# The depthwise convolution of q, k and v on TensorE instead of VectorE, in a macaron block on eight cores

## The chip, the cores and the metric

The kernel runs on all 8 cores of one Trainium2 chip. Each core takes one of the 8 batch elements, runs the same program and exchanges nothing with the others. A time is the device time of the slowest core in microseconds. A core has five engines with an instruction stream each (TensorE, VectorE, ScalarE, GpSimdE, SyncE); they meet only through semaphores. Weights and activations are moved by DMAs, which SyncE, ScalarE or GpSimdE issue.

## The reference

One batch element is x of 2048 x 1024. Three residual steps follow one another: half a feed-forward layer, gated delta attention, half the same feed-forward layer again.

```python
x = x + 0.5 * ffn(layernorm(x))        # complex 512x512 matrix built from two tensor-train cores
x = x + attn(layernorm(x))
x = x + 0.5 * ffn(layernorm(x))

def attn(x):                           # T=2048, D=1024, H=16 heads of 64
    q, k, v = x @ Wq.T, x @ Wk.T, x @ Wv.T
    q, k, v = causal_depthwise_conv(q, cq_w, cq_b), ...   # 4 taps for each channel, plus bias
    g, beta = log_sigmoid(x @ Wg.T), sigmoid(x @ Wb.T)
    k = k / norm(k);  q = q * 64 ** -0.5
    for t:                             # for each head, S is 64x64
        delta = outer(v_t, k_t) - outer(S k_t, k_t)
        S = exp(g_t) * S + beta_t * delta
        o_t = S q_t
    return o @ Wo.T
```

The change concerns only the second line of `attn`: `y[c, t] = b[c] + sum over j of w[c, j] * x[c, t - 3 + j]`, for 1024 channels of each of q, k and v.

## The kernel before

The program is unrolled and written in one order; each operation is put on its engine's stream with the events it must wait for. The helper `mm` (L250) puts out every matmul and the helper `dma` (L273) every DMA. Each finished instruction adds one to its engine's semaphore: `ET` for TensorE, `EV` for VectorE, `EA` for ScalarE, `EP` for GpSimdE. `s.now(ET)` is the number that `ET` will have when everything put on TensorE's stream so far is done, so a wait for it is a wait for all TensorE work written ahead of that place.

After the first feed-forward stage, the second layer norm and the gates, the attention runs over 4 slabs of 512 time steps. A slab has four steps: `_slab_qkv` (projections and convolution), `_slab_prep` (8 chunks of 64 steps), `_slab_solve` and `_slab_chain` (the recurrence and the output projection, with weights `woT`).

`_slab_qkv` works through 24 tiles: q, k, v, each with 8 tiles `ct` of 128 channels. A tile is

- at an even `ct`, a DMA from GpSimdE's queue of 512 KB of weights, which serve this tile and the next, into one of two ring buffers `wring`. It waits for `s.now(ET)`;
- 8 matmuls of 128x128 by 128x512 into PSUM tile `pp0` or `pp1` in turn. The first waits for the weights and for `s.now(EV)`, `s.now(EP)` and `s.now(EA)` (`dep0`);
- the convolution: VectorE copies the last 3 columns of the slab before from `tails` (L648), copies PSUM to `rawt` in fp32 (L650) and saves the new last 3 columns (L652); ScalarE makes the tap of shift 0 with bias into `cacc` (L659); VectorE adds the other three taps (L662, L665, L668) and casts the sum to bf16 into the strip `qcs`, `kcs` or `vcs` (L671).

Weights and bias of a channel stand in one column each (`c_convw`, `c_convb`), read as an operand of one value per partition.

`_slab_prep` begins on ScalarE's queue with three small DMAs (`tcols2` twice, `lgT2`); VectorE splits `lgT2` into three bf16 parts `lgs` (L718 to L726), TensorE spreads them over `pp3` (24 matmuls), and transposes `kcs` into `pp2`.

Of the kernel before, what the change touches and what calls it, by code (L numbers as in the profile page):

```python
# [9 lines left out]
BF16 = mybir.dt.bfloat16  # L10
AF = mybir.ActivationFunctionType
ALU = mybir.AluOpType
# [95 lines left out]
def hr(h):  # L108
    return 64 * (h % 2)


class MK:
# [47 lines left out]
    def _declare_sbuf(self):  # L160
# [60 lines left out]
        self.msk = self._alias("msk", (128, 512), F32, self.ovl3, 4096)  # L221
        self.sstb = self._alias("sstb", (128, 4 * 256), BF16, self.ovl3, 4096)
        self.ktmb = self._alias("ktmb", (128, 512), BF16, self.ovl2, 4096)
        self.subtmp = self._alias("subtmp", (128, 4 * 16 * 15), BF16, self.ovl3, 6144)
        self.msk2 = self._alias("msk2", (128, 512), F32, self.ovl3, 6144)
        self.rbt = self._alias("rbt", (128, 512), F32, self.ovl4, 0)
# [386 lines left out]
    def _slab_qkv(self, sl):  # L613
        s = self.s
        ev_x2 = self.dma(QS, self.x2s[:],
                         self.scr_x2t[:, :, sl * 512:(sl + 1) * 512]
                         .rearrange("a p c -> p a c"),
                         deps=tuple(self.ev_x2t[sl * 4:sl * 4 + 4]) + (s.now(ET),))
        strips = {"q": self.qcs, "k": self.kcs, "v": self.vcs}
        wbase = {"q": 0, "k": 4, "v": 8}  # L620
        self.ev_strip = {}
        ev_conv_last = None
        for wi, w in enumerate("qkv"):
            wsrc = self.wT[w].rearrange("(j p) c -> p j c", p=128)
            ev_w = {}
            for ct in range(8):
                qt = ct // 2
                slot = self.wring[qt % 2]
                if ct % 2 == 0:
                    ev_w[qt] = self.dma(  # L630
                        QG, slot[:].rearrange("p (j cc) -> p j cc", j=8),
                        wsrc[:, :, qt * 256:(qt + 1) * 256],
                        deps=(s.now(ET),))
                pb = self.pp[ct % 2]
                dep0 = (ev_x2, ev_w[qt], s.now(EV), s.now(EP), s.now(EA))
                ev_last = None
                for j in range(8):
                    c0 = j * 256 + (ct % 2) * 128
                    ev_last = self.mm(
                        pb[:, 0:512], slot[:, c0:c0 + 128],  # L640
                        self.x2s[:, j * 512:(j + 1) * 512],
                        deps=dep0 if j == 0 else (), start=(j == 0), stop=(j == 7))
                tl = self.tails[:, (wi * 8 + ct) * 3:(wi * 8 + ct) * 3 + 3]
                dpre = [ev_conv_last]
                if wi == 0 and ct == 0:
                    dpre += [s.now(ET), self.ev_lgflat, self.ev_tcols,
                             s.now(EV), s.now(EA)]
                e_pref = self.dve(lambda e, tl=tl: e.tensor_copy(self.rawt[:, 0:3], tl),  # L648
                                  deps=dpre)
                e_raw = self.dve(lambda e, pb=pb: e.tensor_copy(  # L650
                    self.rawt[:, 3:3 + 512], pb[:, 0:512]), deps=(ev_last,))
                self.dve(lambda e, tl=tl: e.tensor_copy(tl, self.rawt[:, 512:515]),  # L652
                         deps=(e_raw, e_pref))

                def wc(j_, ct=ct, w=w):
                    cix = ct * 12 + wbase[w] + j_
                    return self.c_convw[:, cix:cix + 1]
                bc = self.c_convb[:, ct * 3 + wi:ct * 3 + wi + 1]
                e_c0 = self.act(lambda e, wc=wc, bc=bc: e.activation(  # L659
                    self.cacc[:], self.rawt[:, 3:515], AF.Identity, bias=bc, scale=wc(3)),  # L660
                    deps=(e_pref, e_raw, self.ev_cs))
                e_c1 = self.dve(lambda e, wc=wc: e.scalar_tensor_tensor(  # L662
                    self.cacc[:], self.rawt[:, 2:514], wc(2), self.cacc[:],
                    ALU.mult, ALU.add), deps=(e_c0,))
                e_c2 = self.dve(lambda e, wc=wc: e.scalar_tensor_tensor(  # L665
                    self.cacc[:], self.rawt[:, 1:513], wc(1), self.cacc[:],
                    ALU.mult, ALU.add), deps=(e_c1,))
                e_c3 = self.dve(lambda e, wc=wc: e.scalar_tensor_tensor(  # L668
                    self.cacc[:], self.rawt[:, 0:512], wc(0), self.cacc[:],
                    ALU.mult, ALU.add), deps=(e_c2,))  # L670
                ev_sp = self.dve(lambda e, w=w, ct=ct, strips=strips: e.tensor_copy(  # L671
                    strips[w][:, ct * 512:(ct + 1) * 512], self.cacc[:]), deps=(e_c3,))
                self.ev_strip[(w, ct)] = ev_sp
                ev_conv_last = ev_sp
        self.ev_strip_done = ev_conv_last
# [17 lines left out]
    def _slab_prep(self, sl):  # L693
# [13 lines left out]
        bd = getattr(self, "bankdep", {})  # L707
        ppK, ppV = self.pp[2], self.pp[3]
        for chl in range(SLAB):
            ch = sl * SLAB + chl  # L710
            ev_tc2a = self.dma(QA, self.tcols2[chl % 2][0:64, :], self.scr_tc[ch],
                               deps=(self.ev_tcols,) + tuple(self.ev_tc2rd[chl % 2]))
# [4 lines left out]
                              deps=(self.ev_lgflat,) + tuple(self.ev_lgt_rd))  # L717
            e_h = self.dve(lambda e: e.tensor_copy(self.lgs[:, 0:64], self.lgT2[:]),  # L718
                           deps=(ev_lgt, self.ev_bc_prev))
            e_h = self.dve(lambda e: e.tensor_sub(  # L720
                self.lgT2[:], self.lgT2[:], self.lgs[:, 0:64]), deps=(e_h,))
            e_h = self.dve(lambda e: e.tensor_copy(self.lgs[:, 64:128], self.lgT2[:]),
                           deps=(e_h,))
            e_h = self.dve(lambda e: e.tensor_sub(
                self.lgT2[:], self.lgT2[:], self.lgs[:, 64:128]), deps=(e_h,))
            e_h = self.dve(lambda e: e.tensor_copy(self.lgs[:, 128:192], self.lgT2[:]),  # L726
                           deps=(e_h,))
            self.ev_lgt_rd = (e_h,)
            ev_bc = None
            for pa in range(8):  # L730
                for k3 in range(3):
                    ev_bc = self.mm(
                        ppV[:, pa * 64:pa * 64 + 64],
                        self.c_selb[:, pa * 128:(pa + 1) * 128],
                        self.lgs[:, k3 * 64:k3 * 64 + 64],
                        deps=(e_h, self.ev_ppV_rd, bd.get("pO2"))
                        if pa == 0 and k3 == 0 else (),
                        start=(k3 == 0), stop=(k3 == 2))
            self.ev_bc_prev = ev_bc
            ev_lgrow = self.act(lambda e: e.activation(self.lgrow[:], ppV[:], AF.Copy),  # L740
                                deps=(ev_bc,) + tuple(self.ev_lgrd))
            ev_lg = (ev_lgrow,)
            ev_kt = []
            for h in range(H):
                r0 = hr(h)
                dep = (self.ev_strip[("k", h // 2)],)
                if h == 0:
                    dep += (self.ev_ppK_rd, bd.get("pO1"))
                ev_kt.append(self.mm(
                    ppK[r0:r0 + 64, (h // 2) * 64:(h // 2) * 64 + 64],  # L750
                    self._kc(h, chl, self.kcs), self.c_i64d[r0:r0 + 64, :],
                    deps=dep, tp=(r0, r0)))
            ev_ktmb = self.dve(
                lambda e: e.tensor_copy(self.ktmb[:], ppK[:]),
                deps=(ev_kt[-1], s.now(ET)) + tuple(self.ev_ktm_rd) if chl == 0
                else (ev_kt[-1], self.ev_kc_prev) + tuple(self.ev_ktm_rd))
            ev_sq = self.act(lambda e: e.activation(self.ksq[:], ppK[:], AF.Square),
                             deps=(ev_ktmb, self.ev_ksq_rd))
# [14 lines left out]
                deps=ev_lg + (ev_lnrn,))  # L773
            ev_ms, ev_Es, ev_khs, ev_ts, rdt = [], [], [], [], []
            for par in range(2):
                def tc(c0, par=par, chl=chl):
# [5 lines left out]
                    deps=ev_tc2 + (ev_lnrn,))  # L782
# [3 lines left out]
                                 deps=(ev_m,))  # L786
                ee3 = self.dve(lambda e, cp=cp: e.tensor_scalar_mul(cp(2), cp(8), -1.0),
                               deps=(ev_e1,))
# [4 lines left out]
                    bias=self.cst[par * 64:par * 64 + 64, 2:3]), deps=(ev_lnrn,))  # L793
# [7 lines left out]
                               deps=(ee4,) + ev_lg)  # L801
# [10 lines left out]
                deps=tuple(ev_khs) + (ev_ktmb,))  # L812
# [5 lines left out]
                deps=(ev_rn, self.ev_kc_prev if chl else s.now(ET)))  # L818
            ev_kc = None
            for h in range(H):  # L820
# [6 lines left out]
                    deps=(ev_dgr, ev_ktmb, ev_sq) if h == 0 else (), tp=(r0, r0))  # L827
# [6 lines left out]
            for h in range(H):  # L834
                r0 = hr(h)
                dep = (self.ev_strip[("v", h // 2)],)
                if h == 0:
# [4 lines left out]
                    deps=dep, tp=(r0, r0)))  # L842
# [3 lines left out]
            for h in range(H):  # L846
# [4 lines left out]
                    deps=(ev_kce,) if h == 0 else (), tp=(r0, r0))  # L851
            for h in range(H):
# [4 lines left out]
                    deps=(ev_vtm,) if h == 0 else (), tp=(r0, r0))  # L857
# [10 lines left out]
                deps=ev_lg + tuple(ev_ms) + (s.now(EV),))  # L868
# [3 lines left out]
                          deps=(e3,))  # L872
            e5 = self.dve(lambda e, chl=chl, mskt=mskt, ppK=ppK: e.tensor_mul(
                self.mps2[chl % 2][:], mskt[:], ppK[:]),
                deps=(e4, ev_g) + tuple(self.ev_mp_out[chl % 2]))
# [6 lines left out]
                          deps=(f2,))  # L882
# [457 lines left out]
```

How the kernel before makes its waits and increments, by code:

```python
    def replay(self, eng_name, eng):  # L98
        for item in self.prog[eng_name]:
            if item[0] == "w":
                eng.wait_ge(self.sems[item[1]], item[2])
            elif item[0] == "i":
                item[1](eng).then_inc(self.sems[item[2]], item[3])
            else:
                item[1](eng)
```

## Time and profile before

| | us |
|---|---|
| median of 3 runs | 4031.08 (4020.88 to 4033.50) |
| profiled execution, its own time | 4025.85 |
| span of its slowest core | 4024.0 |
| spans of the eight cores | 3994.8 to 4024.0 |
| PE busy | 1249.0 (31%) |
| DVE busy | 1336.4 (33%) |
| ACT busy | 420.5 (10%) |
| POOL busy | 232.1 (6%) |

PE is TensorE's matmuls, PEld its weight loads, DVE VectorE, ACT ScalarE, POOL GpSimdE, SP SyncE; ACTq is the issue of a DMA by ScalarE. The mean granted clock of TensorE was 0.559 to 0.562 of full speed on every core, where 0.5 is 1.2 GHz and 1.0 is 2.4 GHz. No engine is busy for more than a third of the span. Slab 1, from which most rows below are, has its 24 tiles between 1353 and 1583 us; over the four slabs there are 96 tiles.

### The profile page before, as it was taken

How to read it: one execution, taken by the hardware profiler on the slowest of the kernel's cores; microseconds unless marked ns; L12 is line 12 of the kernel's file. 1: busy time of each engine (PE TensorE's matmuls, PEld its weight loads, DVE VectorE, ACT ScalarE, POOL GpSimd, SP SyncE). 2: the span in 40 equal slices, each digit the busy share in tenths (PEclk: the TensorE clock that was granted, in tenths of full speed). 3: DMA queues.
4: the chain of work that ended last, by engine and by line, in shares of the span. 5: the costliest groups of instructions: out<-in, count | busy, mean ns of one | idle time of the engine just before them, and what ended most of it. 6: DMA issues, size and time to landing. Idle time of an engine off the chain costs nothing.

```text
span 4024.0 us, 35646 instructions; the slowest of 8 cores (3994.8 to 4024.0 us)
## 1 busy us (share of the span) xinstructions
PE 1249.0 (31%) x12112; PEld 619.4 (15%) x12112; DVE 1336.4 (33%) x2703; ACT 420.5 (10%) x1161; POOL 232.1 (6%) x314
## 2 busy tenths in 40 slices
PE   1553323311243333113343321033333210343254
PEld 0121001111121111102120111031101110221011
DVE  2222213444521244453122444531134444321221
ACT  0225100021000001210000011000000110000021
POOL 2000000000100000001000000100000001000100
PEclk9775555555555555555555555555556555555576
DMA  4002112201612221015213210332222108112102
GB/s 129 0 0 53 34 28 26 27 8 11 19 27 37 47 27 23 8 10 20 42 27 47 27 19 9 23 9 37 37 42 27 15 10 24 19 30 37 42 1 84
DMA packets 284802, 114.94 MB, mean 29 GB/s; under 512 B 203280, under 2 KB 260768, under 8 KB 284608
## 3 DMA queue, kind: packets, MB, share of 16 engines
q0 software_dynamic: 139504, 70.91, 17.1%
q1 hardware_dynamic: 112224, 32.70, 3.5%
q10 hardware_dynamic: 32896, 9.05, 1.1%
q8 instruction: 100, 1.64, 0.2%
q14 instruction: 78, 0.64, 0.1%
HBM read 147.46 MB, written 26.08 MB: 43 GB/s over the span
## 4 chain that ended last, share of the span: by engine, by line
PE 30%; DVE 25%; DMA 23%; issue 12%; ACT 6%; ACTq 2%; POOL 1%; DVEq 1%; SPq 1%; POOLq 0%
PE pp L250 30%; DMA wring<-woT 8%; DMA wring<-wqT 2%; DMA wring<-wvT 2%; DMA wring<-wkT 2%; DVE subtmp L946 2%; DMA scr_tc<-tcst 1%; ACTq L273 1%; DMA lgT<-scr_flat 1%; ACT cacc L659 1%; DVE cacc L953 1%; ACT xTt L458 1%; DVE cacc L662 1%; DVE cacc L665 1%; DVE cacc L668 1%
## 5 line engine op out<-in xcount | busy, mean ns | idle before, releaser
L250 PE MATMUL pp<-x2s,wring 128*128 128x512 bf16 x768 | 338.4, 621 | 583.8 <-DMA wring<-wqT 110.8
L250 PE MATMUL pp<-wring,oT 128*128 128x512 bf16 x256 | 119.4, 621 | 386.8 <-DMA wring<-woT 386.8
L250 PEld LDWEIGHTS pp<-x2s,wring 128*128 128x128 bf16 x768 | 99.7, 139 | 822.3 <-issue 822.3
L650 DVE COPY rawt<-pp 128x512 f32<-128x512 f32 x96 | 66.4, 691 | 404.5 <-PE pp L250 404.5
L659 ACT ACTIVATE cacc<-rawt,cconvb,cconvw 128x512 f32<-128x512 f32 x96 | 78.0, 813 | 1050.8 <-DVE rawt L650 1050.8
L1223 DVE TENSOR_TENSOR R<-R,pp 128x512 f32<-128x512 f32 x32 | 20.6, 684 | 474.9 <-PE pp L250 474.9
L250 PE MATMUL pp<-big,xTt 128*128 128x512 bf16 x512 | 168.7, 490 | 20.0 <-ACT xTt L458 20.0
L250 PE MATMUL pp<-ci,xln 128*128 128x128 bf16 x384 | 79.3, 257 | 305.4 <-ACT xTt L458 248.8
L250 PE MATMUL pp<-stripB,stripA 16*16 16x16 bf16 x2048 | 53.9, 167 | 357.6 <-DMA stripB<-scr_t16t 307.6
L1172 ACT ACTIVATE Sb<-Sm 128x512 bf16<-128x512 f32 x32 | 20.1, 629 | 1329.0 <-DVE Sm L1169 1329.0
L250 PE MATMUL pp<-rbf,t32t 32*32 32x64 bf16 x512 | 116.1, 227 | 84.8 <-DVE rbf L1131 84.8
L482 DVE SCALAR_TENSOR_TENSOR R<-pp,R 128x512 f32<-128x512 f32 x64 | 44.3, 692 | 292.8 <-PE pp L250 292.8
L250 PE MATMUL pp<-lgs,cselb 16*128 16x64 bf16 x768 | 45.9, 235 | 298.7 <-DVE lgs L726 298.7
L250 PE MATMUL pp<-rbf,pxs 64*32 64x64 bf16 x512 | 118.8, 232 | 0.0
L250 PEld LDWEIGHTS pp<-stripB,stripA 16*16 16x16 bf16 x2048 | 51.2, 84 | 360.4 <-issue 360.4
L250 PE MATMUL pp<-dgr,ktmb 64*64 64x64 bf16 x512 | 20.4, 238 | 269.6 <-DVE dgr L814 269.6
L250 PEld LDWEIGHTS pp<-wring,oT 128*128 128x128 bf16 x256 | 27.8, 127 | 466.0 <-issue 466.0
L662 DVE SCALAR_TENSOR_TENSOR cacc<-rawt,cconvw,cacc 128x512 f32<-128x512 f32 x96 | 72.2, 752 | 58.8 <-ACT cacc L659 58.8
L250 PEld LDWEIGHTS pp<-ci,xln 128*128 128x128 bf16 x384 | 36.8, 103 | 350.6 <-issue 340.3
L250 PEld LDWEIGHTS pp<-lgs,cselb 16*128 16x128 bf16 x768 | 41.7, 123 | 304.7 <-issue 304.7
L1149 DVE CAST ubf<-pp 128x512 bf16<-128x512 f32 x32 | 22.1, 692 | 173.4 <-PE pp L250 173.4
L273 POOL DMA_DIRECT2D wring<-woT x64 | 46.5, 726 | 570.9 <-PE pp L250 555.9
(154 smaller groups left out, 2439.8 us busy)
## 6 DMA issues: line engine op xcount, KB each, us to landing
wring<-woT POOLq DMA_DIRECT2D x64, 512.0 KB, 5.2
x2s<-scr_x2t SPq DMA_DIRECT2D x8, 1024.0 KB, 7.2
wring<-wqT POOLq DMA_DIRECT2D x16, 512.0 KB, 5.7
wring<-wkT POOLq DMA_DIRECT2D x16, 512.0 KB, 5.7
wring<-wvT POOLq DMA_DIRECT2D x16, 512.0 KB, 5.7
out<-R SPq DMA_DIRECT2D x16, 512.0 KB, 6.9
R<-x ACTq DMA_DIRECT2D x8, 512.0 KB, 11.7
R<-x POOLq DMA_DIRECT2D x8, 512.0 KB, 9.7
```

The source lines that it names most:

```text
L250: return e.matmul(out, lhsT, rhs, start=start, stop=stop, tile_position=tp)
L273: return e.dma_start(out=out, in_=in_)
L458: lambda e, j=j, par=par, pslc=pslc: e.activation(self.xTt[par][:, j * 128:(j + 1) * 128], pslc, AF.Copy),
L482: lambda e, pb=pb, i=i, half=half: e.scalar_tensor_tensor(self.Rt[i][:, half * 512:(half + 1) * 512], pb[:, 0:512], 0.5, self.Rt[i][:, hal ...
L650: e_raw = self.dve(lambda e, pb=pb: e.tensor_copy(self.rawt[:, 3:3 + 512], pb[:, 0:512]), deps=(ev_last,))
L659: e_c0 = self.act(lambda e, wc=wc, bc=bc: e.activation(self.cacc[:], self.rawt[:, 3:515], AF.Identity, bias=bc, scale=wc(3)), deps=(e_pref ...
L662: e_c1 = self.dve(lambda e, wc=wc: e.scalar_tensor_tensor(self.cacc[:], self.rawt[:, 2:514], wc(2), self.cacc[:], ALU.mult, ALU.add), deps ...
L665: e_c2 = self.dve(lambda e, wc=wc: e.scalar_tensor_tensor(self.cacc[:], self.rawt[:, 1:513], wc(1), self.cacc[:], ALU.mult, ALU.add), deps ...
L668: e_c3 = self.dve(lambda e, wc=wc: e.scalar_tensor_tensor(self.cacc[:], self.rawt[:, 0:512], wc(0), self.cacc[:], ALU.mult, ALU.add), deps ...
L946: return e.tensor_mul(ov, tv, mv)
L953: return e.reduce_sum(ov, iv, mybir.AxisListType.X)
L1149: evU = self.dve(lambda e: e.tensor_copy(self.ubf[:], pU[:]), deps=(evA,))
```

## The change

The convolution becomes four matmuls. For each tile ScalarE copies PSUM to `rawtb` in bf16 behind the 3 saved columns, then makes four 128x128 matrices in `dgwb`, the identity times the column of one tap's weights. TensorE multiplies each with `rawtb` shifted by 0 to 3 columns and sums the four products in PSUM tile `pp2` or `pp3`. ScalarE reads that with the bias into the bf16 strip. VectorE keeps only the two small copies of the 3 columns. `dgwb` has two halves that alternate from tile to tile; it lies in memory that is free in this stage, `rawtb` where `rawt` was. `cacc` is no longer used for the convolution. Since `pp2` and `pp3` belong to `_slab_prep` next, its first matmuls into them also wait for the last strips of v.

```diff
+        self.rawtb = self._alias("rawtb", (128, 516), BF16, self.rawt, 0)
+        self.dgwb = self._alias("dgwb", (128, 1024), BF16, self.ovl4, 4096)
...
-                dpre = [ev_conv_last]
+                u = wi * 8 + ct
+                dgw = self.dgwb[:, (u % 2) * 512:(u % 2) * 512 + 512]
+                dpre = [self.ev_tapmm[(u - 1) % 2] if u else None]
...
-                e_raw = self.dve(lambda e, pb=pb: e.tensor_copy(
-                    self.rawt[:, 3:3 + 512], pb[:, 0:512]), deps=(ev_last,))
+                e_raw = self.act(lambda e, pb=pb: e.activation(
+                    self.rawtb[:, 3:3 + 512], pb[:, 0:512], AF.Copy),
+                    deps=(ev_last, self.ev_tapmm[(u - 1) % 2] if u else None))
...
-                e_c0 = self.act(lambda e, wc=wc, bc=bc: e.activation(
-                    self.cacc[:], self.rawt[:, 3:515], AF.Identity, bias=bc, scale=wc(3)),
-                    deps=(e_pref, e_raw, self.ev_cs))
-                e_c1 = self.dve(lambda e, wc=wc: e.scalar_tensor_tensor(
-                    self.cacc[:], self.rawt[:, 2:514], wc(2), self.cacc[:],
-                    ALU.mult, ALU.add), deps=(e_c0,))
...
-                ev_sp = self.dve(lambda e, w=w, ct=ct, strips=strips: e.tensor_copy(
-                    strips[w][:, ct * 512:(ct + 1) * 512], self.cacc[:]), deps=(e_c3,))
+                for k in range(4):
+                    ev_dg.append(self.act(
+                        lambda e, k=k, dgw=dgw, wc=wc: e.activation(
+                            dgw[:, k * 128:(k + 1) * 128], self.c_i128[:],
+                            AF.Copy, scale=wc(k)),
+                        deps=(self.ev_cs, self.ev_tapmm[u % 2]) if k == 0 else ()))
+                pc = self.pp[2 + ct % 2]
+                for k in range(4):
+                    ev_tap = self.mm(
+                        pc[:, 0:512], dgw[:, k * 128:(k + 1) * 128],
+                        self.rawtb[:, k:k + 512],
+                        deps=(ev_dg[-1], e_raw, e_pref,
+                              self.ev_tapev[ct % 2]) if k == 0 else (),
+                        start=(k == 0), stop=(k == 3))
+                self.ev_tapmm[u % 2] = ev_tap
+                ev_sp = self.act(lambda e, w=w, ct=ct, strips=strips, pc=pc,
+                                 bc=bc: e.activation(
+                    strips[w][:, ct * 512:(ct + 1) * 512], pc[:, 0:512],
+                    AF.Identity, bias=bc), deps=(ev_tap,))
+                self.ev_tapev[ct % 2] = ev_sp
```

The waits `dep0` of a tile's first matmul and `deps=(s.now(ET),)` of the weight DMA are written as they were. The order of instructions on TensorE, at the change from one pair of tiles to the next (`wring0` and `wring1` are the ring buffers, `pp` the PSUM tiles, a bracket what an instruction waits for, `qg1` the weight DMA). Before:

```order
L250 MATMUL pp1<-x2s,wring0 128x512 [waits ev,ea]
L250 MATMUL pp1<-x2s,wring0 128x512 x7
L250 MATMUL pp0<-x2s,wring1 128x512 [waits qg1,ev,ea]
L250 MATMUL pp0<-x2s,wring1 128x512 x7
L250 MATMUL pp1<-x2s,wring1 128x512 [waits ev,ea]
```

The same place on TensorE in the changed program:

```order
L252 MATMUL pp1<-x2s,wring0 128x512 [waits ev,ea]
L252 MATMUL pp1<-x2s,wring0 128x512 x7
L252 MATMUL pp3<-rawtb_70,dgwb_71 128x512 [waits ea,ev]
L252 MATMUL pp3<-rawtb_70,dgwb_71 128x512 x3
L252 MATMUL pp0<-x2s,wring1 128x512 [waits qg1,ev,ea]
L252 MATMUL pp0<-x2s,wring1 128x512 x7
L252 MATMUL pp2<-rawtb_70,dgwb_71 128x512 [waits ea,ev]
```

Four tap matmuls now stand between one tile's eight and the next tile's eight, and so ahead of the place at which the weight DMA takes its `s.now(ET)`.

ScalarE's stream at the end of a slab's tiles and the beginning of `_slab_prep`, before:

```order
L659 ACTIVATE cacc<-rawt,cconvb,cconvw 128x512 [waits ev] x24
L273 DMA tcols2_0<-scr_tc 64x96 [waits qa0,qs6]
L273 DMA tcols2_0<-scr_tc 64x96 [waits qa1]
L273 DMA lgT2<-scr_flat 16x64 [waits qa2,qs7]
L740 ACTIVATE lgrow<-pp3 128x512 [waits et]
```

and in the changed program, from the last but one strip on:

```order
L685 ACTIVATE vcs_64<-pp2,cconvb 128x512 [waits et]
L657 ACTIVATE rawtb_70<-pp1 128x512 [waits et]
L670 ACTIVATE dgwb_71<-ci128,cconvw 128x128 x4
L685 ACTIVATE vcs_64<-pp3,cconvb 128x512 [waits et]
L275 DMA tcols2_0<-scr_tc 64x96 [waits qa0,qs6]
L275 DMA tcols2_0<-scr_tc 64x96 [waits qa1]
L275 DMA lgT2<-scr_flat 16x64 [waits qa2,qs7]
```

A tile has one ScalarE instruction before and six now. The four matrices stand behind the copy of PSUM, and the three DMAs behind the last strip, whose instruction waits for the taps.

## Rows read from the trace of the kernel before

**Rows 1.** The chain that ended last: shares of the span by engine.

```profile
PE 30%; DVE 25%; DMA 23%; issue 12%; ACT 6%; ACTq 2%; POOL 1%; DVEq 1%; SPq 1%; POOLq 0%
```

**Rows 2.** What TensorE waited for, whole span: us in total, times, longest.

```profile
PE pp L250 <- DMA wring<-wqT: 110.8, 15, 10.9
PE pp L250 <- DMA wring<-wkT: 108.8, 16, 8.0
PE pp L250 <- DMA wring<-wvT: 107.4, 16, 7.3
PE pp L250 <- DVE kcs L671: 81.2, 16, 5.4
```

**Rows 3.** Timeline, two tiles of slab 1: start, duration, instruction [idle before <-releaser].

```profile
1400.01 3.52 PE L250 MATMUL pp<-x2s,wring 128*128 128x512 bf16 x8 [6.47 <-DMA wring<-wqT]
...
1403.64 0.69 DVE L650 COPY rawt<-pp 128x512 f32<-128x512 f32 x1 [5.02 <-PE pp L250]
1404.43 0.81 ACT L659 ACTIVATE cacc<-rawt,cconvb,cconvw 128x512 f32<-128x512 f32 x1 [9.18 <-DVE rawt L650]
...
1407.91 0.43 DVE L671 CAST qcs<-cacc 128x512 bf16<-128x512 f32 x1
...
1408.59 3.57 PE L250 MATMUL pp<-x2s,wring 128*128 128x512 bf16 x8 [5.05 <-DVE qcs L671]
...
1412.70 0.87 POOL L273 DMA_DIRECT2D wring<-wqT  x1 [17.73 <-PE pp L250]
...
1418.60 3.57 PE L250 MATMUL pp<-x2s,wring 128*128 128x512 bf16 x8 [6.44 <-DMA wring<-wqT]
```

**Rows 4.** ScalarE's instructions grouped by form, whole span: busy, mean ns | idle before.

```profile
L659 ACT ACTIVATE cacc<-rawt,cconvb,cconvw 128x512 f32<-128x512 f32 x96 | 78.0, 813 | 1050.8 <-DVE rawt L650 1050.8
L508 ACT ACTIVATE xTt<-pp 128x128 bf16<-128x128 f32 x128 | 29.0, 272 | 16.2 <-PE pp L250 16.0 <-issue 0.2
L1172 ACT ACTIVATE Sb<-Sm 128x512 bf16<-128x512 f32 x32 | 20.1, 629 | 1329.0 <-DVE Sm L1169 1329.0
L740 ACT ACTIVATE lgrow<-pp 128x512 f32<-128x512 f32 x32 | 19.1, 597 | 206.9 <-PE pp L250 206.9
L791 ACT ACTIVATE cc<-tcols,cst 64x8 f32<-64x8 f32 x64 | 18.5, 290 | 0.0
L789 ACT ACTIVATE cc<-tcols 64x8 f32<-64x8 f32 x64 | 12.7, 198 | 0.1
```

**Rows 5.** Timeline, ScalarE back to back in the first chunk of slab 1.

```profile
1595.02 0.20 ACT L789 ACTIVATE cc<-tcols 64x8 f32<-64x8 f32 x1
1595.12 0.29 ACT L791 ACTIVATE cc<-tcols,cst 64x8 f32<-64x8 f32 x1
```

**Rows 6.** Timeline, ScalarE to TensorE, and four and eight matmuls in a row.

```profile
1350.83 1.86 PE L250 MATMUL pp<-wring,oT 128*128 128x512 bf16 x4 [6.39 <-DMA wring<-woT]
...
3803.51 1.90 PE L250 MATMUL pp<-big,xTt 128*128 128x512 bf16 x8
...
3812.85 0.45 ACT L458 ACTIVATE xTt<-pp 128x128 bf16<-128x128 f32 x2 [0.33 <-PE pp L250]
...
3813.55 1.86 PE L250 MATMUL pp<-big,xTt 128*128 128x512 bf16 x4 [0.62 <-ACT xTt L458]
```

**Rows 7.** Timeline, last tile of slab 1 and the beginning of the preparation.

```profile
1577.57 3.49 PE L250 MATMUL pp<-x2s,wring 128*128 128x512 bf16 x8 [5.05 <-DVE vcs L671]
...
1581.95 0.81 ACT L659 ACTIVATE cacc<-rawt,cconvb,cconvw 128x512 f32<-128x512 f32 x1 [7.73 <-DVE rawt L650]
...
1582.02 1.11 ACTq L273 DMA_DIRECT2D tcols<-scr_tc  x2
...
1583.22 0.54 ACTq L273 DMA_DIRECT2D lgT<-scr_flat  x1
...
1585.78 0.17 DVE L718 CAST lgs<-lgT 16x64 bf16<-16x64 f32 x1
...
1587.30 1.43 PE L250 MATMUL pp<-lgs,cselb 16*128 16x64 bf16 x24 [6.24 <-DVE lgs L726]
...
1588.89 0.60 ACT L740 ACTIVATE lgrow<-pp 128x512 f32<-128x512 f32 x1 [6.12 <-PE pp L250]
```

**Rows 8.** Stretches: length, busy us of PE, PEld, DVE, ACT, POOL; PEclk, DMA share, GB/s.

```profile
1353.00:1583.00 230.00, 84.12 (x192) 24.94 (x192) 90.61 (x167) 19.51 (x24) 10.51 (x12) 0.59 0.23 32
...
1403.36:1406.77 3.41, 0.17 (x1) 0.00 (x0) 2.19 (x4) 0.81 (x1) 0.00 (x0) 1.00 0.00 0
1406.77:1410.18 3.41, 1.59 (x4) 0.57 (x5) 1.53 (x4) 0.00 (x0) 0.00 (x0) 0.50 0.00 0
```

**Rows 9.** DMA issues: KB each, median us from issue to landing.

```profile
lgT<-scr_flat ACTq DMA_DIRECT2D x32, 4.0 KB, 1.7
```

More of the change, by code:

```diff
@@ L621, in _slab_qkv @@
         self.ev_strip = {}
+        if not hasattr(self, "ev_tapmm"):
+            self.ev_tapmm = [None, None]
+            self.ev_tapev = [None, None]
         ev_conv_last = None
@@ L647, in _slab_qkv @@
                              s.now(EV), s.now(EA)]
-                e_pref = self.dve(lambda e, tl=tl: e.tensor_copy(self.rawt[:, 0:3], tl),
-                                  deps=dpre)
-                e_raw = self.dve(lambda e, pb=pb: e.tensor_copy(
-                    self.rawt[:, 3:3 + 512], pb[:, 0:512]), deps=(ev_last,))
-                self.dve(lambda e, tl=tl: e.tensor_copy(tl, self.rawt[:, 512:515]),
+                e_pref = self.dve(lambda e, tl=tl: e.tensor_copy(
+                    self.rawtb[:, 0:3], tl), deps=dpre)
+                e_raw = self.act(lambda e, pb=pb: e.activation(
+                    self.rawtb[:, 3:3 + 512], pb[:, 0:512], AF.Copy),
+                    deps=(ev_last, self.ev_tapmm[(u - 1) % 2] if u else None))
+                self.dve(lambda e, tl=tl: e.tensor_copy(tl, self.rawtb[:, 512:515]),
                          deps=(e_raw, e_pref))
@@ L658, in _slab_qkv @@
                 bc = self.c_convb[:, ct * 3 + wi:ct * 3 + wi + 1]
-                e_c0 = self.act(lambda e, wc=wc, bc=bc: e.activation(
-                    self.cacc[:], self.rawt[:, 3:515], AF.Identity, bias=bc, scale=wc(3)),
-                    deps=(e_pref, e_raw, self.ev_cs))
-                e_c1 = self.dve(lambda e, wc=wc: e.scalar_tensor_tensor(
-                    self.cacc[:], self.rawt[:, 2:514], wc(2), self.cacc[:],
-                    ALU.mult, ALU.add), deps=(e_c0,))
[L665 to L670, printed above, removed]
-                ev_sp = self.dve(lambda e, w=w, ct=ct, strips=strips: e.tensor_copy(
-                    strips[w][:, ct * 512:(ct + 1) * 512], self.cacc[:]), deps=(e_c3,))
+                ev_dg = []
+                for k in range(4):
[5 more added lines that the diff above has]
+                pc = self.pp[2 + ct % 2]
+                ev_tap = None
+                for k in range(4):
[11 more added lines that the diff above has]
+                self.ev_tapev[ct % 2] = ev_sp
                 self.ev_strip[(w, ct)] = ev_sp
@@ L735, in _slab_prep @@
                         self.lgs[:, k3 * 64:k3 * 64 + 64],
-                        deps=(e_h, self.ev_ppV_rd, bd.get("pO2"))
+                        deps=(e_h, self.ev_ppV_rd, bd.get("pO2"),
+                              self.ev_strip[("v", 7)])
                         if pa == 0 and k3 == 0 else (),
@@ L747, in _slab_prep @@
                 if h == 0:
-                    dep += (self.ev_ppK_rd, bd.get("pO1"))
+                    dep += (self.ev_ppK_rd, bd.get("pO1"),
+                            self.ev_strip[("v", 6)])
                 ev_kt.append(self.mm(
```

## The prediction

> **What bounds the kernel now.** I began with the chain that ended last, since no engine is busy for more than a third of the span. It is shared out among TensorE, VectorE and DMAs [rows 1]: work that follows on other work, so what counts is the length of the steps and not the load of an engine. Next, what TensorE waited for. The weights of q, k and v hold it for 110.8 + 108.8 + 107.4 = 327 us in 47 waits, and the cast of the last tile's strip for about 80 us in each of q, k and v (the row of k stands there) [rows 2]. Both are in the stage that the change touches.
>
> The timeline shows how these waits arise [rows 3]. After an even tile, TensorE's eight matmuls end at 1400.01 + 3.52 = 1403.53, VectorE, ScalarE and VectorE make the convolution until 1408.34, and the next burst starts at 1408.59, a gap of 5.06 us. After an odd tile the burst ends at 1408.59 + 3.57 = 1412.16, and there the weight DMA leaves, at 1412.70; the next burst starts at 1418.60, a gap of 6.44 us. The convolution of that tile ends about 1.4 us before the weights are there. So the convolution sets the gap after even tiles and the load, counted from TensorE's last instruction, the gap after odd ones.
>
> **What is removed and added on the path.** The convolution's waits stay: a burst still waits for everything that ScalarE and VectorE did before, so tiles do not overlap. The gap after an even tile becomes a chain of six ScalarE instructions and four matmuls:
>
> - From the end of a burst to ScalarE's start 0.16 us (1587.30 + 1.43 = 1588.73 to 1588.89) [rows 7].
> - The copy of PSUM to bf16: 0.597 us, as L740, which reads a PSUM tile of the same size [rows 4].
> - One matrix: no row shows it. 128x128 from PSUM without a pointer operand takes 0.272. Reading SBUF instead adds 629 - 597 = 0.032, and one pointer operand 290 - 198 = 0.092, together 0.396 us; by the same steps L659 comes out at 629 + 2 x 92 = 813, which is what it took [rows 4]. Back to back, ScalarE starts the next instruction 0.10 us before the last one ends (0.198 long, next start after 0.10) [rows 5]. Copy and four matrices: 0.497 + 3 x 0.296 + 0.396 = 1.78 us. The matrices need nothing from this tile, but stand behind the copy on ScalarE's stream, which waits for the burst, so all four lie on the path. Below, 0.272 each is the bound (0.50 us less a tile, 48 us in all); above, 0.396 with no overlap (0.40 more, 38 us in all).
> - ScalarE's end to TensorE's start: 3812.85 + 0.45 = 3813.30 to 3813.55, 0.25 us [rows 6].
> - Four tap matmuls of 512 columns at 1.2 GHz: 1.86 us [rows 6].
> - To ScalarE again 0.16, the strip 0.597 + 0.092 for the bias = 0.69, to TensorE 0.25.
>
> From the burst's end to the end of the taps: 0.16 + 1.78 + 0.25 + 1.86 = 4.05 us. With the strip, 5.15 us against 5.06: what VectorE gives up, ScalarE and TensorE take. 48 such gaps x 0.09 = +4 us.
>
> By the Trainium skill (ScalarE: Activation LUTs, What ACT_TABLE_LOAD costs) a matrix would take 186 + 93 + 0.833 x 128 = 386 ns, an estimate from its figures; the sum would fall by 4 us.
>
> **What is moved.** This is the large term. The weight DMA waits for all TensorE work written ahead of it, and the taps of the odd tile are now written ahead of it. It can leave only when they end, 4.05 us after the burst instead of at once. From there it takes the 6.44 us that the trace shows from TensorE's last matmul to the next burst [rows 3], and the strip and its semaphore (1.10 us) hide behind it. The gap is 4.05 + 6.44 = 10.49 us, +4.05. There are 11 such gaps in a slab, since the first load of a slab follows on no tile: 44 x 4.05 = +178 us. Behind the waiting DMA on GpSimdE's queue stands nothing that is needed sooner.
>
> At a slab's end the three small DMAs on ScalarE's queue stand behind the last strip, as its order shows. Before, the last burst ended at 1577.57 + 3.49 = 1581.06, ScalarE's instruction started at 1581.95, the DMAs 0.07 later, `lgT2`'s 1.20 after that, and the spreading matmuls at 1587.30, 6.24 us after the burst [rows 7]. After: the strip starts at 4.05 + 0.16 = 4.21, `lgT2`'s DMA 1.27 later at 5.48, it lands after 1.7 [rows 9] at 7.18, and VectorE's five instructions with the hop to TensorE take 1587.30 - 1585.78 = 1.52: 8.70 us, +2.46. Four times: +10 us. Before, VectorE was still at the taps when `lgT2` landed; now it is free and waits for it. The added waits for the strips of v cost nothing: the last strip is done at 4.21 + 0.69 = 4.90 us, the matmul that waits for it starts at 8.70.
>
> VectorE's two small copies are beside the burst and ScalarE's matrices. Their waits hold up nothing: behind them on VectorE's stream stand only the next tile's copies.
>
> **The clock.** In slab 1 the granted clock was 0.59 in the mean, so at full level for 0.18 of 230 us, 41 us. One stretch at full level began at 1403.36, at the end of a burst, and ended at 1406.77, 3.41 us later [rows 8], so there were 12 in 24 tiles. Before, nothing ran in them. The taps would run from 2.19 to 4.05 us after the burst's end, and that stretch reached until 3.24. At full level eight matmuls took 1.90 us and not 3.57; four more cost half of 3.57 - 1.86 = 1.71, so four take about 1.90 - 0.86 = 1.04, 0.82 less [rows 3, 6]. They would just fit. I take 0.45 of the tiles, a little under half since some stretches will end too early: 96 x 0.45 x 0.82 = -35 us. Bounds: none of the tiles (+35), all (-43 more).
>
> **Sum.** 4 + 178 + 10 - 35 = +157 us. On the profiled execution's 4025.85 us that gives 4183, and the median of the runs shown lies 5 us above it: 4188 us. The stages outside keep their instructions.
>
> **Rivals.**
>
> *The clock holds through the short gaps.* TensorE's pauses within a pair are now 2.19 and 1.10 us, not 5.06. If the full level outlasts them, then in the 0.45 of pairs where it begins with the even tile the odd burst takes 1.90 instead of 3.57 and its taps are sure to be fast: 48 x 0.45 x (1.67 + 0.55 x 0.82) = -46, so 4142 us. For it: the pauses are shorter than any in this stage so far. Against: in the stretch after that full level TensorE was idle for all but 0.17 us before [rows 8], so the trace does not test it; the taps add only some 1 us there. Its own chance 0.12. The Trainium skill (TensorE: Matmul & The Clock Gate, Why this matters for your kernels) says that the clock is lost by idle gaps over about 3 us between bursts. By that rule the pair would keep it. The trace agrees only as far as the 5 us gap, after which the level had fallen.
>
> *The taps are slower than other matmuls.* Two of four read `rawtb` from an odd column, 2 bytes off; no matmul in the trace does. If each of them took a second pass of 1.71 / 4 = 0.43 us: 96 x 2 x 0.43 = +82, so 4270 us. Nothing speaks for it but that it is new. Chance 0.08.
>
> *The load is not held back.* The other side: if the weight DMA left with the burst's end as now, the gap after odd tiles would be the greater of 6.44 and 5.15, +0, and the sum 4 + 10 - 35 = -21: 4010 us, 0.5% faster than the median. It needs that `s.now(ET)` doesn't count the taps; it is read when the next even tile is written, after them, and the order has them there. The load must not be held by more than about 0.48 us a gap (21 / 44) for the change to win. Chance 0.03. A clock at full level in every burst would also turn the sign, 96 x 1.67 + 53 x 0.82 = -203 more, 3985 us, but it would have to survive gaps of 10 us; 0.01.
>
> *Part of the load's wait is hidden*, by a shorter landing or by slower cores of the eight setting the time, enough to end within 0.3%: 0.03.
>
> **How the numbers follow.** The forecast has 0.73. Its own range is 4140 to 4226: the matrix's bounds, -48 and +38. With the clock's bounds (-43 and +35) and the first rival's 4142, 8 times in 10 hold 4135 to 4250; the slow taps stay outside. I count 0.3%, 12 us, as what a measurement can tell from no change. Faster: 0.03 + 0.01 = 0.04. Within 0.3%: 0.03. Slower: 0.73 + 0.12 + 0.08 = 0.93.
>
> **What the profile would show.** TensorE's wait for the three weights: counted from the end of the taps, about 6.4 us each and 47 times, little changed in sum; and about 44 gaps of 10.5 us from eight matmuls to the next eight. A slab's tiles take (178 + 4 - 35) / 4 = 37 us more, about 266 instead of 230. ScalarE's matrices at 0.39 to 0.40 us each, 384 of them, 150 us busy more. The taps as 384 matmuls, four in 1.86 or about 1.04 us. VectorE is busy 96 x (0.69 + 3 x 0.75 + 0.43) = 324 us less, and the time gains nothing by it. PEclk in the tiles near 0.59. I am wrong if weight DMAs leave before the taps, if a burst overlaps another tile's ScalarE work, or if bursts run in 1.9 us.

## The result, and the profile after

The changed kernel takes 4152.47 us in the median of 8 runs (4145.57 to 4163.58), the kernel before 4032.29 in 8: a ratio of 1.0302 (95% interval 1.0284 to 1.032), 3.0% slower. The forecast was 4188 us within 4135 to 4250. The profiled execution took 4156.18 us; the span of its slowest core, core 1, is 4154.6.

The chain that ended last in the changed kernel, against [rows 1]:

```profile
PE 32%; DMA 23%; DVE 20%; issue 12%; ACT 9%; ACTq 2%; POOL 1%; DVEq 1%; SPq 1%; POOLq 0%
```

VectorE gave up 5 points of a longer span, ScalarE and TensorE took them. VectorE is busy for 1000.9 us where it was busy for 1336.4, and the kernel is slower all the same. The same view of TensorE's waits as [rows 2]:

```profile
PE pp L252 <- ACT dgwb L670: 204.2, 96, 2.4
PE pp L252 <- DMA wring<-wkT: 110.2, 16, 7.7
PE pp L252 <- DMA wring<-wqT: 109.5, 15, 9.5
PE pp L252 <- DMA wring<-wvT: 109.1, 16, 7.1
...
PE pp L252 <- ACT qcs L685: 14.9, 16, 0.9
```

The weights still hold TensorE for 329 us in 47 waits, where it was 327 before. The sum is unchanged and hides the loss, for the waits after odd tiles now begin when the taps are done. Before, the other waits were for the last strip; beside k's in [rows 2] stand those of v and q, in all 239.5 us in 47 waits, 5.10 us each:

```profile
PE pp L250 <- DVE vcs L671: 81.2, 16, 5.4
PE pp L250 <- DVE qcs L671: 77.1, 15, 5.4
```

Here are two tiles of slab 1 in the timeline, the view of [rows 3]; a burst is a tile's eight matmuls:

```profile
1413.55 0.69 ACT L685 ACTIVATE qcs<-pp,cconvb 128x512 bf16<-128x512 f32 x1 [1.37 <-PE pp L252]
...
1414.38 3.26 PE L252 MATMUL pp<-x2s,wring 128*128 128x512 bf16 x8 [0.93 <-ACT qcs L685]
...
1417.74 0.60 ACT L657 ACTIVATE rawtb<-pp 128x512 bf16<-128x512 f32 x1 [3.50 <-PE pp L252]
1418.23 1.27 ACT L670 ACTIVATE dgwb<-ci,cconvw 128x128 bf16<-128x128 bf16 x4
...
1419.76 1.06 PE L252 MATMUL pp<-rawtb,dgwb 128*128 128x512 bf16 x4 [2.11 <-ACT dgwb L670]
1420.92 0.69 ACT L685 ACTIVATE qcs<-pp,cconvb 128x512 bf16<-128x512 f32 x1 [1.41 <-PE pp L252]
...
1421.37 0.87 POOL L275 DMA_DIRECT2D wring<-wqT  x1 [22.72 <-PE pp L252]
...
1427.54 3.51 PE L252 MATMUL pp<-x2s,wring 128*128 128x512 bf16 x8 [6.72 <-DMA wring<-wqT]
```

The burst of an odd tile ends at 1417.64, its taps at 1420.82; only then, at 1421.37, does the weight DMA leave, and the next burst starts at 1427.54, 9.90 us after the end of the last one, where it was 6.44. From the first burst's start to the end of its last taps slab 1 takes 252.6 us; before, to the end of its last burst, it took 218.4. The instructions grouped by form:

```profile
L252 PE MATMUL pp<-x2s,wring 128*128 128x512 bf16 x768 | 335.8, 616 | 384.5 <-DMA wring<-wkT 110.2 <-DMA wring<-wqT 109.5 <-DMA wring<-wvT 109.1
...
L252 PE MATMUL pp<-rawtb,dgwb 128*128 128x512 bf16 x384 | 127.4, 465 | 204.2 <-ACT dgwb L670 204.2
...
L670 ACT ACTIVATE dgwb<-ci,cconvw 128x128 bf16<-128x128 bf16 x384 | 122.0, 392 | 0.0
```

A tile's taps keep TensorE busy for 127.4 / 96 = 1.33 us and start 204.2 / 96 = 2.13 us after the burst. The end of slab 1, which answers to [rows 7]:

```profile
1652.62 3.57 PE L252 MATMUL pp<-x2s,wring 128*128 128x512 bf16 x8 [0.93 <-ACT vcs L685]
...
1659.42 0.69 ACT L685 ACTIVATE vcs<-pp,cconvb 128x512 bf16<-128x512 f32 x1 [1.37 <-PE pp L252]
...
1660.68 0.53 ACTq L275 DMA_DIRECT2D lgT<-scr_flat  x1
...
1664.32 1.43 PE L252 MATMUL pp<-lgs,cselb 16*128 16x64 bf16 x24 [4.99 <-DVE lgs L742]
```

The spreading matmuls start 8.1 us after the end of the last burst; over the four slabs of this core it is 7.9 to 8.1 us.

### The profile page after: what moved, and what is told of

Read it like the earlier page. It is cut to its first block, busy times and chain, and to the rows that moved or that the text cites. A ratio compares the mean times of both kernels' runs of the same rounds, so it can differ in the third digit from the quotient of the medians.

```text
span 4154.6 us, 36230 instructions; the slowest of 8 cores (4120.8 to 4154.6 us)
## 1 busy us (share of the span) xinstructions
PE 1376.9 (33%) x12496; PEld 653.1 (16%) x12496; DVE 1000.9 (24%) x2223; ACT 579.4 (14%) x1641; POOL 232.2 (6%) x314
## 4 chain that ended last, share of the span: by engine, by line
PE 32%; DMA 23%; DVE 20%; issue 12%; ACT 9%; ACTq 2%; POOL 1%; DVEq 1%; SPq 1%; POOLq 0%
PE pp L252 32%; DMA wring<-woT 8%; ACT dgwb L670 3%; DMA wring<-wqT 2%; DMA wring<-wvT 2%; DMA wring<-wkT 2%; DVE subtmp L964 2%; ACT rawtb L657 1%; DMA lgT<-scr_flat 1%; DMA scr_tc<-tcst 1%; ACTq L275 1%; DMA wb<-scr_w 1%; DVE cacc L971 1%; ACT xTt L460 1%; DMA x2s<-scr_x2t 1%
## 5 line engine op out<-in xcount | busy, mean ns | idle before, releaser
L252 PE MATMUL pp<-x2s,wring 128*128 128x512 bf16 x768 | 335.8, 616 | 384.5 <-DMA wring<-wkT 110.2
L252 PE MATMUL pp<-wring,oT 128*128 128x512 bf16 x256 | 119.4, 621 | 392.0 <-DMA wring<-woT 392.0
L252 PE MATMUL pp<-rawtb,dgwb 128*128 128x512 bf16 x384 | 127.4, 465 | 204.2 <-ACT dgwb L670 204.2
L660 DVE CAST tails<-rawtb 128x3 f32<-128x3 bf16 x96 | 16.3, 169 | 727.0 <-ACT rawtb L657 693.6
L657 ACT ACTIVATE rawtb<-pp 128x512 bf16<-128x512 f32 x96 | 57.7, 601 | 861.4 <-PE pp L252 861.4
L252 PE MATMUL pp<-stripB,stripA 16*16 16x16 bf16 x2048 | 53.9, 167 | 348.8 <-DMA stripB<-scr_t16t 299.1
L670 ACT ACTIVATE dgwb<-ci,cconvw 128x128 bf16<-128x128 bf16 x384 | 122.0, 392 | 0.0
L252 PEld LDWEIGHTS pp<-rawtb,dgwb 128*128 128x128 bf16 x384 | 34.6, 106 | 314.7 <-issue 299.6
```

Of the source, the lines that this page charges most:

```text
L252: return e.matmul(out, lhsT, rhs, start=start, stop=stop, tile_position=tp)
L657: e_raw = self.act(lambda e, pb=pb: e.activation(self.rawtb[:, 3:3 + 512], pb[:, 0:512], AF.Copy), deps=(ev_last, self.ev_tapmm[(u - 1) % ...
L660: self.dve(lambda e, tl=tl: e.tensor_copy(tl, self.rawtb[:, 512:515]), deps=(e_raw, e_pref))
L670: lambda e, k=k, dgw=dgw, wc=wc: e.activation(dgw[:, k * 128:(k + 1) * 128], self.c_i128[:], AF.Copy, scale=wc(k)),
```

## The experiments

All times are medians. Each ratio is to the kernel before, run on the same chip; there it took 4024 to 4026 us and not the 4032 of the result above. The changed kernel itself was not run beside the experiments, so a difference from it is read from the ratios, times 4025 us.

**1. The load no longer held by the taps.** `ev_burst` keeps the event of each tile's eighth matmul, and the load waits for the last of them.

```diff
-                        deps=(s.now(ET),))
+                        deps=(ev_burst[-1] if ev_burst else et0,))
```

> The changed kernel, but the weight load waits for the eight matmuls of the tile before and no longer for its taps. Theory (the load held back by the taps is the price): the gap after odd tiles falls from 10.3 us to the 6.7 us that it had before the change, the gap after even tiles stays at 4.4 us; 44 x 3.6 = 158 us less, about 3994 us, under the kernel before, since the even gaps are shorter than before (5.1). Rival (the price is the added work of ScalarE and TensorE itself, and the load is hidden beside it): the odd gap stays above 10 us and the time at 4150 us.

It takes 3993.85 us, ratio 0.9926 (0.9907 to 0.9944). TensorE's waits:

```profile
PE pp L252 <- DMA wring<-wqT: 64.2, 15, 9.9
PE pp L252 <- DMA wring<-wvT: 51.7, 16, 3.7
PE pp L252 <- DMA wring<-wkT: 50.3, 16, 4.7
```

166 us of the 329 are left, 163 less, and the ratio fell from 1.0302 to 0.9926, which is 151 us (159 between the medians). This one wait was more than the whole loss: without it the taps on TensorE are 0.7% ahead of the kernel before.

**2. The load ahead**, in the changed kernel and, as experiment 4, in the kernel before: it waits for the last reader of its ring buffer.

```diff
-                        deps=(s.now(ET),))
+                        deps=(ev_burst[-3] if len(ev_burst) >= 4 else et0,))
```

> The changed kernel, but the weight load waits only for the last matmuls that read its ring buffer, one pair of tiles earlier. Theory: the odd gap is then set by the convolution's chain as the even one, 4.4 us instead of 10.3; 44 x 5.9 = 260 us less, about 3892 us. Rival (the load takes longer beside matmuls and ScalarE's work, or a second wait stands behind it): the odd gap ends at 6 us or more, 3965 us or more.

It takes 3900.68 us, ratio 0.9691 (0.9672 to 0.9709), where 3892 was foreseen.

**3. The matrices first**: the loop over the four matrices is moved ahead of the copy of PSUM on ScalarE's stream, and the first matrix of a slab also waits for the work written ahead of the slab; the load is as in the changed kernel.

> The changed kernel, but ScalarE makes a tile's four matrices before it copies PSUM, so beside the burst; the weight load waits as in the changed kernel. Theory (the matrices lie on the path only because of their place in ScalarE's order): from a burst's end to its taps 1.0 us instead of 2.1, in all 96 tiles: 107 us less, about 4045 us, give or take 15 us for the share of taps at full clock. Rival (the taps wait for something else, such as their operands' last writes): under 30 us less, 4120 us or more.

It takes 4068.72 us, ratio 1.0111 (1.0087 to 1.0135): 77 us less than the changed kernel by the ratios (84 between the medians), and not 107. The wait before the taps fell as foreseen, from 204 to 92 us:

```profile
L252 PE MATMUL pp<-rawtb,dgwb 128*128 128x512 bf16 x384 | 169.9, 592 | 91.8 <-ACT rawtb L673 86.3 <-DVE tails L676 5.5
```

The taps however took 169.9 us and not 127.4, 1.77 us a tile, so most of them ran at half clock. Over the six cores whose records of these matmuls are complete the mean rose from 127 to 163 us. That their place in ScalarE's order put the matrices on the path is shown; 37 of the 112 us that this gave went to the clock. Core 1 of the same execution tells more. Each stretch runs from the start of a slab's first burst to the end of its last taps, so its length is measured (columns as in [rows 8]):

```profile
582.96:806.72 223.76, 114.09 (x288) 32.36 (x288) 8.19 (x48) 57.17 (x139) 9.63 (x11) 0.61 0.21 26
1364.89:1581.61 216.72, 106.25 (x288) 31.20 (x288) 8.20 (x48) 57.17 (x139) 9.61 (x11) 0.67 0.22 27
2139.87:2376.31 236.44, 126.75 (x288) 34.40 (x288) 8.19 (x48) 57.17 (x139) 9.61 (x11) 0.53 0.19 25
2935.77:3175.49 239.72, 129.62 (x288) 34.76 (x288) 8.19 (x48) 57.17 (x139) 9.62 (x11) 0.51 0.19 24
```

The same 288 matmuls and the work around them took 217 and 224 us where the granted clock was 0.67 and 0.61, and 236 and 240 us where it was 0.53 and 0.51.

**4. The load ahead in the kernel before.**

> The kernel before the change, with the weight load waiting only for the last matmuls that read its ring buffer. Theory: the gap after odd tiles falls from 6.7 us to the 5.1 us of the convolution on VectorE; 44 x 1.6 = 71 us less, about 3960 us. With the load out of the way the changed convolution should be ahead of this by 96 x 0.7 = 67 us. Rival (the load still ends last): no change, 4030 us.

It takes 3953.08 us, ratio 0.9826 (0.9805 to 0.9847), where 3960 was foreseen. Experiment 2, on the same chip, is 52 us below it: with the load out of both, the change gains, a little less than the 67 foreseen.

**5. Both edits, 2 and 3.**

> The changed kernel with both edits, the load ahead and the matrices ahead of the copy, in the order of tiles as it is. If the two add up: 3900 us less the 1.1 us that the matrices leave in each of 96 gaps, 106 us, about 3795 us. If the taps lie at half clock, as in most slabs with the matrices first alone, 96 x 0.4 = 40 us of that are lost, 3835 us.

It takes 3644.64 us, ratio 0.9062 (0.9044 to 0.9079): 253 us under edit 2 alone by the ratios (256 between the medians), where 106 were foreseen. The timeline of core 1 shows why:

```profile
1361.48 3.21 PE L252 MATMUL pp<-x2s,wring 128*128 128x512 bf16 x8 [0.93 <-ACT vcs L690]
...
1372.39 1.89 PE L252 MATMUL pp<-x2s,wring 128*128 128x512 bf16 x8 [0.93 <-ACT vcs L690]
...
1375.22 1.02 PE L252 MATMUL pp<-rawtb,dgwb 128*128 128x512 bf16 x4 [0.95 <-ACT rawtb L673]
...
1377.18 1.89 PE L252 MATMUL pp<-x2s,wring 128*128 128x512 bf16 x8 [0.93 <-ACT vcs L690]
```

Most bursts take 1.89 us: at the full clock, which here holds over pauses of 0.95 and 0.93 us. Every few bursts one falls back, as the one of 3.21 us. With edit 2 alone the pauses are 2.10 and 0.93 us (core 2):

```profile
1412.18 3.21 PE L252 MATMUL pp<-x2s,wring 128*128 128x512 bf16 x8 [0.93 <-ACT qcs L688]
...
1417.50 1.11 PE L252 MATMUL pp<-rawtb,dgwb 128*128 128x512 bf16 x4 [2.10 <-ACT dgwb L673]
...
1419.53 3.57 PE L252 MATMUL pp<-x2s,wring 128*128 128x512 bf16 x8 [0.93 <-ACT kcs L688]
```

There the bursts take 3.2 to 3.6 us. By groups, on the slowest core of each, the bursts fell from 330.9 us (752 matmuls recorded) to 222.7 (768), the taps from 126.4 (376 recorded) to 103.4 (384) and their wait from 204.7 to 91.8, together 244 us. So 113 us are the pauses themselves and some 130 the clock.

**6. Another order.** Edits 2 and 3, and a tile's taps stand behind the next tile's burst, which waits only for what it reads and overwrites. **7.** is the kernel before with edit 2 and that same `dep0`, which is the part of the edit that both have:

```diff
-                dep0 = (ev_x2, ev_w[qt], s.now(EV), s.now(EP), s.now(EA))
+                dep0 = (ev_x2, ev_w[qt], bar0,
+                        ev_rd[-2] if len(ev_rd) >= 2 else None)
```

> The changed kernel with the load ahead and the matrices first, and in another order: a tile's taps stand behind the next tile's eight matmuls, and a burst waits only for its weights and for the copy that frees its PSUM tile, not for all of ScalarE and VectorE. Theory (what the change adds is small once nothing waits in turn): a tile costs TensorE its burst and its taps, and the load of a pair, 6.4 us from the last reader's end, sets a pair at 6.5 to 7 us instead of 21; a slab's tiles take 90 us instead of 245, about 3540 us. If TensorE's clock stays at half level, a pair takes 2 x (3.5 + 1.8) = 10.6 us and the time is 3680 us. Rival (loads from HBM on eight cores at once, or ScalarE's 2.6 us a tile, bind): 3750 us or more.

> The kernel before the change with the load ahead and the same freedom: a burst waits only for its weights and for the copy that frees its PSUM tile. Theory: the tile is then bound by VectorE and ScalarE in turn, about 5.0 us from copy to copy as the trace of before shows, 120 us for a slab's tiles instead of 219: about 3635 us. The difference from the reordered changed kernel, some 95 us in favour of the taps on TensorE, is what the change is worth where nothing else waits. Rival (VectorE is not the bound): as fast as the reordered changed kernel.

6 takes 3423.23 us, ratio 0.8506 (0.8494 to 0.8519), and 7 takes 3623.29 us, ratio 0.9002 (0.8989 to 0.9016). The first is 15% below the kernel before, and it came out 117 us under its forecast. A pair of tiles takes 5.9 us here, and a slab's tiles 69 to 71 us where 90 were foreseen. The bursts take 1.89 us, at the full clock, and a load leaves while the one before it is still on its way, as the DMA at 601.38 ahead of the wait that ends at 601.89:

```profile
601.38 0.87 POOL L275 DMA_DIRECT2D wring<-wqT  x1 [4.31 <-PE pp L252]
...
601.89 1.89 PE L252 MATMUL pp<-x2s,wring 128*128 128x512 bf16 x8 [0.19 <-DMA wring<-wqT]
...
603.61 1.03 PE L252 MATMUL pp<-rawtb,dgwb 128*128 128x512 bf16 x4
604.48 1.89 PE L252 MATMUL pp<-x2s,wring 128*128 128x512 bf16 x8
...
606.20 1.03 PE L252 MATMUL pp<-rawtb,dgwb 128*128 128x512 bf16 x4
...
607.80 1.89 PE L252 MATMUL pp<-x2s,wring 128*128 128x512 bf16 x8 [0.57 <-DMA wring<-wqT]
```

In 7, VectorE's copies of PSUM follow one another every 4.90 us, so its chain is the bound, as foreseen:

```profile
1359.90 0.69 DVE L656 COPY rawt<-pp 128x512 f32<-128x512 f32 x1
...
1364.80 0.69 DVE L656 COPY rawt<-pp 128x512 f32<-128x512 f32 x1
```

A slab's tiles take 109 to 111 us there, where 120 were foreseen. The two differ by 200 us, where some 95 were foreseen. So moving the convolution off VectorE, worth 52 us where the tiles take turns (2 against 4), is worth 200 where they overlap.

**8. Three small loads on SyncE.**

> The changed kernel, but the three small loads of a slab's first chunk are issued by SyncE instead of ScalarE. Theory (they are late because they stand behind the last strip on ScalarE's stream): from the last burst's end to the spreading matmuls about 5 us (the last strip done at 4.3 us or so) instead of 8.0. Rival (VectorE or TensorE sets that gap): it stays at 8 us. In the whole time 12 us at most, less than one look can tell; the gap in the trace decides.

This is slab 0's end in that kernel, on core 5:

```profile
825.03 3.42 PE L252 MATMUL pp<-x2s,wring 128*128 128x512 bf16 x8 [0.93 <-ACT vcs L685]
...
832.50 1.44 PE L252 MATMUL pp<-lgs,cselb 16*128 16x64 bf16 x24 [0.93 <-ACT vcs L685]
```

The last burst ends at 828.45, and the spreading matmuls start 4.05 us later, where the changed kernel has about 8.0 (4.05 or 4.06 in all four slabs): the place on ScalarE's queue was the cause. The spreading matmuls now wait for the last strip. The single time, 4120.17 us, decides nothing.

**9 to 11. Does added work move the clock?** Into the kernel of experiment 3 comes one copy by ScalarE in odd tiles, whose result nothing uses, on the path to the taps. It is 128x128 in 9 and 128x512 in 10; 11 has none: it is the kernel of experiment 3 once more, on the chip of 9 and 10.

```diff
+                if ct % 2 == 1:
...
+                    ev_dg.append(self.act(lambda e, oth=oth, src=src: e.activation(
+                        oth, src, AF.Copy), deps=(e_raw, ev_dg[-1])))
```

> The kernel with the matrices first, and one more ScalarE copy of 128x128 between the copy of PSUM and the taps of each odd tile, about 0.35 us on the path of 48 tiles; its result is used by nothing. Theory A (in that kernel the tiles settle into one of two rhythms, a pair in 17.05 us with the odd burst and the taps at full clock, or in 20.5 us at half clock, and stay there; added work shifts the rhythm): the share of fast pairs changes, and the time with it by much more than the added work, either way; if the tiles no longer settle, pairs of both kinds mix in every slab and the time falls below that of the kernel without the copy, perhaps 4030 us. Theory B (the clock is chance from tile to tile): 48 x 0.35 = 17 us slower than the kernel without the copy.

> The same with a copy of 128x512, about 0.7 us on the path of 48 tiles. Theory A: again another share of fast pairs, so a time that is not the added work's. Theory B: 48 x 0.7 = 34 us slower than the kernel without the copy.

> The kernel with the matrices first once more, on the chip of the two others: about 1.0111 of the kernel before, 4069 us where that takes 4024.

The ratios are 1.0136 (1.0119 to 1.0153) for 9, 1.0097 (1.0071 to 1.0124) for 10, and 1.0109 (1.0092 to 1.0126) for 11. The groups of 10 (core 6) and then of 11 (core 5), each the slowest core:

```profile
L252 PE MATMUL pp<-x2s,wring 128*128 128x512 bf16 x768 | 323.5, 597 | 385.0 <-DMA wring<-wqT 112.6 <-DMA wring<-wvT 108.5 <-DMA wring<-wkT 107.3
L252 PE MATMUL pp<-rawtb,dgwb 128*128 128x512 bf16 x384 | 138.7, 499 | 125.9 <-ACT dgwb L679 80.1 <-ACT rawtb L673 42.7 <-DVE tails L681 3.2
```

```profile
L252 PE MATMUL pp<-x2s,wring 128*128 128x512 bf16 x768 | 339.8, 622 | 385.5 <-DMA wring<-wkT 110.5 <-DMA wring<-wvT 110.5 <-DMA wring<-wqT 109.7
L252 PE MATMUL pp<-rawtb,dgwb 128*128 128x512 bf16 x384 | 166.5, 583 | 91.6 <-ACT rawtb L673 86.2 <-DVE tails L676 5.5
```

On these two cores the long copy adds 34 us of waiting before the taps, and the matmuls give back 16 + 28 = 44. But cores of one execution differ much in this: without a copy the taps took from 127 us (core 1) to 167 us (core 0). The six cores whose records are complete, in the mean, with the clock granted in all four runs of each kernel:

| | bursts, us | taps, us | wait before the taps, us | granted clock |
|---|---|---|---|---|
| 11, no copy | 328.0 | 154.6 | 91.8 | 0.554 |
| 9, short copy | 330.4 | 147.9 | 110.7 | 0.558 |
| 10, long copy | 321.6 | 133.6 | 126.0 | 0.567 |

The long copy adds 34 us of waiting to a core and the matmuls give back 27, most of it in the taps. The time of the slowest core is 5 us less by the ratios, inside the intervals, where by theory B the ratio would be 1.019; the mean span of a core is 6 us more (4049.9 against 4043.5). The short copy adds 19 us of waiting and its matmuls give back 4, less than the cores differ by; it cost 11 us, near theory B's 17. That added work moves the clock is shown for 10. The strong form of theory A, that it makes the kernel faster, is not shown, for 9 nothing is, and what in the rhythm of pauses and work the clock follows stays open.

## Why the prediction was right, and where its sizes were off

The direction, the place and the cause were right; the sum, +157 us, was too large, and each of the terms below was put too high. Between the two profiled executions lie 130 us, between the medians 120.

- **The moved load** was put at +178, less 16 for fast taps (44 x 0.45 x 0.82), so +162. Measured, the taps and their wait in 44 gaps are 44 x (2.13 + 1.33) = 152, and the waits for weights grew by 2: +154. Experiment 1 gives it by itself, 151 us by the ratios.
- **Even gaps** were put at +4, less 18 for the clock (48 x 0.45 x 0.82), so -14. Measured: 2.13 + 1.33 + 0.93 = 4.39 us against 5.10 before, so 48 x -0.71 = -34. This is the term mis-sized most. Two of its sizes were wrong. From the last tap to the next burst the hops between engines were taken from other places, 0.16 and 0.25 us round a strip of 0.69, and are 0.10 (1420.82 to 1420.92) and 0.14 (1414.24 to 1414.38): 0.93 us and not 1.10. And taps at full clock were put at 0.45 of the tiles; by (1.86 - 1.33) / (1.86 - 1.02) it is 0.63. Why it is more, the runs don't settle.
- **The matrices** take 392 ns each (0.396 us foreseen) and four of them 1.27 us; the path from burst to taps is 2.13 us (2.19 foreseen). Experiment 3 shows the place in ScalarE's order as the cause.
- **The slab's end** was put at +2.46 us each. It is 8.0 us against 6.24, +7 in all. Experiment 8 shows the cause.
- 154 - 34 + 7 - 3 for slightly shorter bursts = 124. The other 6 us are not pinned down: outside these terms TensorE's waits moved both ways, for `woT` from 386.8 to 392.0 us, for `xTt` (L458, L460) from 268.8 to 277.8, for `stripB` from 307.6 to 299.1.

**The rivals.** *The load is not held back* fell by the timeline: the DMA leaves at 1421.37, after the taps' end at 1420.82. *The taps are slower than other matmuls* fell: four of them take 1.02 to 1.06 us at full clock, or 1.86 us at half (experiment 3, most tiles), as [rows 6] has for four others. *Part of the load's wait is hidden* fell, with 329 us of waits against 327. *The clock holds through the short gaps* fell for the changed kernel, whose bursts take 335.8 us (338.4 before), with pauses of 2.13 and 0.93 us. The mechanism itself is real: in experiment 3 it came in part of the slabs and in 5 in most bursts, with pauses of 0.95 and 0.93 us within a pair. The Trainium skill (TensorE: Matmul & The Clock Gate, Why this matters for your kernels) names idle gaps over about 3 us between bursts as what to avoid. That section does not say that shorter gaps keep the clock, as the prediction took it, and experiment 2 shows that they need not: between 1386 and 1436 us on core 2, with pauses of 2.10 and 0.93 us and no wait for a load between, the bursts took 3.2 to 3.6 us. That the pauses move the clock is shown by 2 against 5, and not always in the same sense, as 10 shows, where a longer pause came with a higher clock. By what rule is not shown.

## What to carry to other kernels

A wait written as "everything so far on that engine" changes its meaning when instructions are put ahead of it: look for every such wait behind an insertion, and let it name the instruction that it needs. Work that moves to another engine gains little while the engines wait in turn (52 us here, against 200 once the tiles overlap); remove the waiting first, and only then ask which engine is the bound. Within a chain, put what does not depend on the step ahead of what does, and look at the clock afterwards: in experiment 5 pauses shorter by 113 us brought 253, while in 3 the clock took back 37 of 112.

## What the runs showed of the hardware that was not expected

- Shortening one of two pauses from 2.10 to 0.95 us took bursts of eight from 3.2 to 3.6 us to mostly 1.89 us (experiments 2 and 5), worth some 130 us beyond the pause itself.
- With load gaps of about 6.8 us still there (experiment 3), slabs of equal instructions took from 217 to 240 us, by the clock they were granted, 0.67 to 0.51.
- 34 us of ScalarE work added to the path of a core came with a higher granted clock, 0.567 against 0.554, and matmuls 27 us shorter (experiments 10 and 11).
